# Three r buffers and two bank pairs in the first pass, a new order of its work, fewer stashes early, and a later finish in attention

## The reference

```
h = relu(layernorm(x))                       # per row
# layer 0
score = sum(h[src] * h[dst]);  a = softmax of score over the edges of one dst
agg = segment_sum((h @ W_conv + b_conv)[src] * a, dst)
out = agg + relu(h @ W_res + b_res)          # r = the second term, for all nodes
x = x + batchnorm(out)                       # mean and variance over all 100,000 rows
# layer 1
h = relu(layernorm(x))
m = gelu(gelu([h[src], h[dst], edge_attr] @ W_m1 + b_m1) @ W_m2 + b_m2)
boxes = segment_sum(m, dst)
x = x + gelu(gelu([h, boxes] @ W_c1 + b_c1) @ W_c2 + b_c2)
```

## Time and profile before

| what | value |
|---|---|
| median of 3 runs | 1633.65 us (1632.19 to 1642.5) |
| the profiled execution | 1630.99 us, of which the span of its instructions is 1629.2 us |
| first pass, until VectorE's last instruction of it | 0 to 312.2 us |
| VectorE idle until the first edge rows are there | 312.2 to 329.3 us |
| attention and the batch norm's numbers | 329.3 to 722.5 us |
| dense pass | 722.5 to about 1180 us |
| edge pass | about 1180 to 1629 us |
| VectorE busy in the first pass, in attention | 260.16 of 312.2 us, 340.65 of 393.2 us |
| TensorE's granted clock in the two | 0.83, 0.76 of full speed |

### The profile page before, as it was taken

One profiled execution on the slowest core, in us unless ns is written; L12 is line 12 of the kernel. 1 busy time (PEld: TensorE's weight loads), 2 busy tenths in 40 slices (PEclk: granted clock), 3 DMA queues, 4 the chain that ended last, 5 costly groups with the idle time before them and its releaser, 6 DMA issues.

```text
span 1629.2 us, 21884 instructions
## 1 busy us (share of the span) xinstructions
PE 1290.4 (79%) x6227; PEld 777.5 (48%) x6227; DVE 1234.1 (76%) x2432; ACT 945.8 (58%) x1647; POOL 1093.4 (67%) x989
## 2 busy tenths in 40 slices
PE   4566665558778778767999989999969999999983
PEld 2233332247666667654545444444444454554431
DVE  8898888488988988866777777777667777777661
ACT  5688786623323323326777777777646676666651
POOL 7788887777777777777776057667735555445355
PEclk8888788757877877878999999999989999999985
DMA  7666675468876543354655467666375454454410
GB/s 211 222 224 195 206 221 199 146 223 294 275 275 221 142 124 115 91 194 139 203 185 192 163 209 230 202 202 201 113 230 151 142 159 133 143 158 130 123 50 16
DMA packets 141969, 287.34 MB, mean 176 GB/s; under 512 B 33104, under 2 KB 50614, under 8 KB 141852
## 3 DMA queue, kind: packets, MB, share of 16 engines
q1 hardware_dynamic: 109532, 255.32, 46.9%
q0 software_dynamic: 32320, 30.62, 8.0%
HBM read 165.47 MB, written 121.80 MB: 176 GB/s over the span
## 4 chain that ended last, share of the span: by engine, by line
PE 47%; DVE 18%; POOL 16%; issue 10%; ACT 6%; DMA 2%; SPq 0%; DVEq 0%; POOLq 0%; ACTq 0%
POOL x_ring L607 8%; POOL gout L607 7%; PE banks L1501 6%; PE banks L1478 6%; PE banks L1525 4%; PE banks L1407 3%; PE banks L1598 3%; PE banks L1596 3%; PE banks L1424 3%; PE banks L1605 3%; PE banks L1511 3%; DVE sums L841 3%; ACT cT L1230 2%; DVE gout L1016 2%; PE banks L1491 2%
## 5 line engine op out<-in xcount | busy, mean ns | idle before, releaser
L607 POOL DMA_INDIRECT agg_ring<-agg_rows,edge_idx x196 | 213.5, 1089 | 161.4 <-DMA edge_agg<-agg_ring 97.5
L611 POOL DMA_INDIRECT out<-agg,put_last x196 | 196.5, 1002 | 184.3 <-DVE agg L1048 129.3
L607 POOL DMA_INDIRECT x_ring<-in_x,edge_idx x200 | 239.2, 1196 | 63.5 <-issue 63.5
L607 POOL DMA_INDIRECT gout<-in_x,edge_idx x192 | 226.2, 1178 | 58.5 <-issue 58.2
L611 POOL DMA_INDIRECT agg_rows<-agg,put_first x196 | 216.9, 1107 | 59.7 <-issue 55.8
L738 DVE TENSOR_REDUCE stat<-sq 128x16 f32<-128x1024 f32 (+1 forms) x98 | 118.7, 1213 | 26.3 <-ACT sq L1093 21.9
L1229 ACT ACTIVATE cT<-banks,packed 96x512 f32<-96x512 f32 (+1 forms) x98 | 66.8, 682 | 107.4 <-PE banks L1501 107.3
L963 DVE TENSOR_TENSOR xc<-banks,xc 128x512 f32<-128x512 f32 (+1 forms) x74 | 51.2, 692 | 92.2 <-PE banks L1525 90.9
L1501 PE MATMUL banks<-hT,packed 64*96 64x512 f32 (+1 forms) x392 | 112.6, 652 | 2.8 <-ACT hT L1222 2.8
L1365 PE MATMUL banks<-ident,xc 128*128 128x128 f32 (+1 forms) x296 | 54.4, 345 | 75.9 <-DVE xc L767 64.9
L1511 PE MATMUL banks<-cT,packed 96*64 96x512 f32 (+1 forms) x392 | 105.5, 616 | 0.4 <-ACT gout L1238 0.4
(11 more groups left out here) (191 smaller groups left out, 3384.8 us busy)
## 6 DMA issues: line engine op xcount, KB each, us to landing
xt<-in_x SPq DMA_DIRECT2D x48, 512.0 KB, 6.1
r_rows<-rT SPq DMA_DIRECT2D x48, 512.0 KB, 7.0
xe<-edge_x SPq DMA_DIRECT2D x96, 256.0 KB, 3.8
agg_rows<-rb SPq DMA_DIRECT2D x48, 512.0 KB
xt<-in_x_t SPq DMA_DIRECT2D x36, 512.0 KB, 5.0
out<-xc SPq DMA_DIRECT2D x36, 512.0 KB, 3.2
edge_r<-rr SPq DMA_DIRECT2D x48, 256.0 KB, 3.8
rT<-r_rows SPq DMA_DIRECT2D x24, 512.0 KB, 5.6
```

The lines of the kernel that those rows point to most:

```text
L607: A.indirect_dma_start(to, None, table[:, :], bass.IndirectOffsetOnAxis(ap=idx, axis=0), bounds_check=limit, oob_is_err=False).then_inc(si ...
L611: A.indirect_dma_start(table[:, :], bass.IndirectOffsetOnAxis(ap=idx, axis=0), rows_of, None, bounds_check=limit, oob_is_err=False).then_i ...
```

## The change

In the first pass r has three buffers instead of two (the third is rb[0]) and three store semaphores. The products of even steps go to the banks W[1], of odd steps to W[3], so `r_product(s)` waits for the relu of s - 2 instead of s - 1. The unread output of `square_r` goes to the banks W[2] instead of SBUF. ACT's work on a pair of r is put off: in pair i it copies, takes the relu of and squares the steps of pair i - 1 in a new order. DVE sums, centres, sums, centres, and polishes after both. SP stores the steps 2i - 3 and 2i - 2 in pair i, and stashes up to group 6i // 7 instead of i + 1, so 20 groups in the first pass instead of 25; in attention it goes on with 6/5 of a group a pair, still with at least 2i + 6. STASH goes from 9 to 12. In attention `edge_finish` of both groups stands behind `invert`.

```
-STASH = 9
+STASH = 12
-        r_junk, zero = rb[0], rb[1]
+        r_ring = rT + rb[0:1]
+        zero = rb[1]
+        r_banks = [W[1], W[3]]
+        r_junk = W[2]
-        A_st = slots("r_stored", 2)
+        A_st = slots("r_stored", 3)
...
# SP, first pass
-                for s in (a - 2, a - 1):
+                for s in (a - 3, a - 2):
                     if is_step(s):
                         store_r(s)
-                due = i + 1
+                due = 6 * i // 7
...
# SP, attention
-            store_r(S - 1)
+            for s in (S - 2, S - 1):
+                store_r(s)
+            before = stashed
             for i in range(PAIRS + 1):
                 a = 2 * i
-                due = min(G, max(PAIRS + 4 * (i + 1) // 3, a + 6))
+                due = min(G, max(before + 6 * (i + 1) // 5, a + 6))
...
# DVE, first pass
                     sum_squares(dstat(1, s, p), sq[s % 2][0:p, :], A_sq, s, A_ss)
-                if is_step(2 * i + 2):
-                    center(2 * i + 2)
+                    if is_step(s + 2):
+                        center(s + 2)
                 polish(i, nodes_of(pair[-1]), 0, R * len(pair))
...
-                if is_step(2 * i + 3):
-                    center(2 * i + 3)
# DVE, attention (edge_center: n == 2 waits for the transposes of S - 2, not S - 1)
-                for n in (a, b):
-                    if is_group(n - 4):
-                        edge_finish(n - 4)
-                    if is_group(n):
-                        p = edges_of(group_of(n))
-                        sum_squares(estat(1, n, p), esq[n % 2][0:p, :], E_sq, n, E_ss)
                 pair = [n for n in (a, b) if is_group(n)]
+                for n in pair:
+                    p = edges_of(group_of(n))
+                    sum_squares(estat(1, n, p), esq[n % 2][0:p, :], E_sq, n, E_ss)
                 if pair:
                     invert(i, P, 2 * R, 2 * R + ER * len(pair), E_inv, E_ss, pair[-1])
+                for n in (a - 4, b - 4):
+                    if is_group(n):
+                        edge_finish(n)
...
# ACT, first pass (relu_r and square_r use r_ring[s % 3] and r_banks[s % 2], wait for s - 3)
             square(0, A_ctr, A_ss, A_sq)
-            for i in range(PAIRS + 1):
+            square(1, A_ctr, A_ss, A_sq)
+            for i in range(PAIRS):
                 a, b = 2 * i, 2 * i + 1
-                if is_step(b):
-                    square(b, A_ctr, A_ss, A_sq)
+                if is_step(a - 2):
+                    copy_hT(a - 2)
+                if is_step(b - 4):
+                    square_r(b - 4)
+                if is_step(b - 2):
+                    copy_hT(b - 2)
                 if is_step(a - 2):
                     relu_r(a - 2)
-                if is_step(a):
-                    last = b if is_step(b) else a
-                    seed_roots(i, nodes_of(last), 0, R * (last - a + 1), last)
+                last = b if is_step(b) else a
+                seed_roots(i, nodes_of(last), 0, R * (last - a + 1), last)
+                if is_step(a + 2):
+                    square(a + 2, A_ctr, A_ss, A_sq)
+                if is_step(b - 2):
+                    relu_r(b - 2)
                 if is_step(a - 2):
                     square_r(a - 2)
-                if is_step(a + 2):
-                    square(a + 2, A_ctr, A_ss, A_sq)
-                if is_step(a - 1):
-                    relu_r(a - 1)
-                    square_r(a - 1)
-                for s in (a, b):
-                    if is_step(s):
-                        copy_hT(s)
+                if is_step(b + 2):
+                    square(b + 2, A_ctr, A_ss, A_sq)
...
# ACT, start of attention
+            copy_hT(S - 1)
+            square_r(S - 2)
             for n in range(2):
                 square_group(n)
+            relu_r(S - 1)
+            square_r(S - 1)
...
# PE (r_product: W[1] becomes r_banks[s % 2])
-                A_relu.part(pe, s - 1, b + 1)
+                A_relu.part(pe, s - 2, b + 1)
...
             pe.wait_ge(s_b, 12)
+            A_relu.done(pe, S - 2)
+            A_rsq.done(pe, S - 1)
```

More of the change, by code:

```diff
@@ L403, in store_r @@
                 p = nodes_of(s)
-                o, i = r_rows[s], rT[s % 2][:, :]
+                o, i = r_rows[s], r_ring[s % 3][:, :]
                 if p != P:
@@ L812, in edge_center @@
                 if n == 2:
-                    A_t.done(dve, S - 1)
+                    A_t.done(dve, S - 2)
                 subtract_mean(ec[n % 4][0:p, :], xe[n % 4][0:p, :], estat(0, n, p), E_ctr, n, 1)
@@ L1111, in relu_r @@
                 p = nodes_of(s)
-                A_st.done(act, s - 2)
-                A_rsq.done(act, s - 2)
+                A_st.done(act, s - 3)
+                A_rsq.done(act, s - 3)
                 for b in range(2):
@@ L1116, in relu_r @@
                     act.wait_ge(A_r.sem, A_r.after(s, b + 1))
-                    A.activation(blocks(rT[s % 2][:, c], p), blocks(W[1][:, c], p), ACT.Relu, bias=bres2[:, :],
+                    A.activation(blocks(r_ring[s % 3][:, c], p), blocks(r_banks[s % 2][:, c], p), ACT.Relu, bias=bres2[:, :],
                                  accum_out=rsum[:, 2 * s + b:2 * s + b + 1]).then_inc(A_relu.sem, 1)
@@ L1123, in square_r @@
                 A_rsq.done(act, s - 1)
[L1124 removed]
+                A.activation(blocks(r_junk[:, :], p), blocks(r_ring[s % 3][:, :], p), ACT.Square,
                              accum_out=rsq[:, s:s + 1]).then_inc(A_rsq.sem, 1)
             square(0, A_ctr, A_ss, A_sq)
[L1128 removed]
+            square(1, A_ctr, A_ss, A_sq)
+            for i in range(PAIRS):
                 a, b = 2 * i, 2 * i + 1
[L1130 to L1131 removed]
+                if is_step(a - 2):
[4 more added lines that the diff above has]
+                    copy_hT(b - 2)
                 if is_step(a - 2):
                     relu_r(a - 2)
[L1134 to L1136 removed]
+                last = b if is_step(b) else a
[4 more added lines that the diff above has]
+                    relu_r(b - 2)
                 if is_step(a - 2):
                     square_r(a - 2)
[L1139 to L1146 removed]
+                if is_step(b + 2):
+                    square(b + 2, A_ctr, A_ss, A_sq)
             def edge_square(n, p, ready, summed, st):
@@ L1372, in r_product @@
                 pe.wait_ge(A_ht.sem, A_ht.after(s, b + 1))
-                A_relu.part(pe, s - 1, b + 1)
-                T.matmul(blocks(W[1][:, c], p), wres2[:, :], blocks(hT2[s % 2][:, c], p), start=True, stop=True)\
+                A_relu.part(pe, s - 2, b + 1)
+                T.matmul(blocks(r_banks[s % 2][:, c], p), wres2[:, :], blocks(hT2[s % 2][:, c], p), start=True, stop=True)\
                  .then_inc(A_r.sem, 1)
```

1 line of the change is left out of this document (removed).

## The result

| kernel | median (lowest to highest, runs) | profiled execution's span |
|---|---|---|
| before | 1632.92 us (1629.95 to 1642.5, 4) | 1629.2 us |
| changed | 1616.36 us (1613.91 to 1619.69, 4) | 1612.1 us |

A forecast was written before the change was run, and what follows sets the result against it. POOL's unpausing gathers, 12.66 us a group with one stash a pair, were taken to bound the first pass. 1630.99 - 35 - 12.7 - 10 = 1573.3 us profiled, so a median of 1576, range 1555 to 1604.

The forecast's parts named there:

- first pass's mechanism: First pass: fewer stashes due let DVE set the pace instead of POOL's gathers; -35 us, bounds -38 and -15.
- under 30: First pass, sign in the trace: SP's waits for gathers under 30 us instead of 171.8.
- 7 us of waits for seeds: First pass: of 42.0 us, about 4.5 stay in the last pair and 2.5 over the others.
- no pair is faster than 12.66 us: First pass before the change: SP stashes one group a pair, and a group's gathers take 12.66 us.
- Handover: From first pass to attention: DVE's 17.10 us wait for the first edge rows shrinks; -12.7 us (-15 to -9).
- Now nothing on SP waits for a gather there: Handover: the first edge rows' loads no longer stand behind stash and gather of the 25th group.
- rival (1): First pass: POOL sets the pace again, a group taking 12.95 us; +12 us, 1588 in total; chance 0.13.
- the lead: First pass: POOL starts more than a group ahead, so its 10.85 us a pair doesn't hold DVE before the last pairs.
- Attention: Attention: moving edge_finish removes DVE's wait for the product; twelve slow pairs at 0.8 us, -10 us, bounds -29 and +10.
- the slack of 0.8 us a slow pair: Attention's slow pairs: PE has half the next scan's transposes at 500.2 us, the scan started at 501.04.
- Cost nothing: Later passes: first stash of sums due at 936 us, when POOL has had its four groups since 906; no cost.
- Dense pass: Dense pass: as long as before, a forecast difference of 0.

The follow-up runs named there:

- g4: Changed kernel with the old pace of gathered groups (one a pair in the first pass, 4/3 in attention): 2044.3 us, 1.014 of the kernel before.
- i3: Changed kernel with a shorter pause after each indirect DMA, STASH 10, and first-pass row sums and roots in PSUM: 1688.1 us, 1.035 of the kernel before.
- g1: The changed kernel itself, nothing altered, on a slower chip: 2047.6 us, 1.022 of the kernel before.
- g2: Changed kernel with STASH 10 in place of 12, on a slower chip: 2021.5 us, 1.012 of the kernel before.
- f2: Changed kernel with first-pass row sums and polished roots in PSUM, so one SBUF input: 2111.9 us, 1.039 of the kernel before.
- f3: Changed kernel with one SBUF input in the first pass and STASH 10: 2096.1 us, 1.031 of the kernel before.
- e3: Changed kernel with edge_finish back in its old place between the square sums: 2063.9 us, 1.024 of the kernel before.
- e2: Changed kernel with STASH 9 as before: 2029.1 us, 1.009 of the kernel before.
- f4: Changed kernel with edge_finish back in its old place, repeated on the second chip: 2082.8 us, 1.025 of the kernel before.
- f1: Changed kernel with STASH 10, on the second chip: 2065.3 us, 1.014 of the kernel before.
- i1: Changed kernel with a shorter pause (memset of 128 x 320) after each indirect DMA, on a chip like the first: 1693.7 us, 1.040 of the kernel before.
- i2: Changed kernel with the shorter pause after each indirect DMA and STASH 10: 1709.2 us, 1.050 of the kernel before.
- e4: The kernel before with STASH 12 alone: 2037.5 us, 1.013 of the kernel before.

## Why the prediction was wrong

- **The first pass's mechanism was right, and its size within the bounds.** 10.36 us a pair against 10.53 worked out, SP's waits for gathers 26.3 against "under 30", none of ACT on r's store in the steady pairs. The 4.3 us that lack are the start and the end: the forecast left 7 us of waits for seeds, and 14.1 are there. From 36.6 to 56 us SP waited 19.6 us for rows that VectorE builds (17.4 before), with r's stores behind it, and VectorE then stood 5.8 us for seeds at 71.4 us (a reach that the forecast didn't follow); the last three pairs' seeds come 1.5, 2.8 and 3.5 us late. g4 shows that none of this gain is there without the pace. One reading of the working is wrong without harm: "no pair is faster than 12.66 us". From 83.3 to 162.8 us the pairs of the kernel before took 11.4 us each; 12.66 is a mean, and the sum used it as one.
- **Handover, -7.9 for -12.7.** "Now nothing on SP waits for a gather there" fell. Gathers were priced at 12.66 us a group as before, but denser two-input instructions hold them longer: 1.41 + 0.30 us, 13.6 us a group. This is rival (1)'s mechanism, at 0.95 us a group and not the 0.29 it was given, and it did not set the steady pace, as the lead covered it until the last pairs. i3 measured what it costs there on the paced kernel: 9.9 us with the end of the first pass.
- **Attention, -3.2 for -10.** That the wait moves to the scan was foreseen; the slack of 0.8 us a slow pair was not there: 22.9 us in 12 waits stand where 24.5 stood. The two-pair period fell from 30.91 to 30.72 us, and a slow pair from 16.64 to 16.47 where 15.8 was forecast. The step priced the slack with TensorE's 14.64 us of the old slow pair, as if the clock there stayed at 0.59. It is 0.53 now, and 14.47 us are busy with fewer products; the clock is lower in the fast pair too (0.94 for 1.00). Why was not tested. The finish in its old place gave 2063.9 and 2082.8 us, ratios of 1.024 and 1.025 where the changed kernel on another chip has 1.022 +-0.012: nothing that these runs can tell, so that no experiment shows what the move is worth.
- **"Cost nothing" for the stashes of sums: the step that failed, and the largest part of the miss.** It asked whether the first stash, at 936 us by its count (956.27 measured), finds its four groups, and stopped there. It had to ask as well whether the last ones are in HBM when the edge pass reads them, a pass that was to begin 58 us earlier: with three groups a pair from 12 instead of 9 the sums came 4.6 us earlier, the pass 35.4. Measured cost +18.3 us, beside 21.9 us more of VectorE's waits for sums. On the slower chips STASH 12 against 9 or 10 costs 27 to 34 us of edge pass: g1/g2 and f2/f3, where nothing else differs and the pass starts within 3 us, and e3/e2, f4/f1, where the finish differs too (and f1's pass starts 27 us later, which takes from the last figure). The pair i1/i2 says nothing of it.
- **Dense pass, +6.4 us**: TensorE's clock there is 0.96 for 0.97, with 8 falls of the clock instead of 4, about 1.6 us each (an estimate from 18 us stretches at a clock of 0.91); TensorE is busy 424.0 us there for 417.5. Why there are more was not tested.

The errors add up: 4.3 + 4.8 + 6.8 + 6.4 + 18.3 = 40.6 us, which is the forecast's distance. Without the edge pass's 18.3 us the forecast would have been 22.3 us off. The changed kernel with STASH at 10 and no pause was never run on a chip like the first; that it would give the 18 us back is argued (GpSimd's ring is full some 18 us after its first gather at 890.5 us, and a first stash two pairs ahead of 956.3 us, at 18.3 us a pair, goes out near 920), not shown. No version beat both kernels on both sorts of chip: the pause wins 0.876 on one and loses 1.040 on the other.

## What to carry to other kernels

When a queue's duty is put off, follow it to both ends: to the first item (is it there when it is due?) and to the last (is it there when it is read?), and find who stands with a full buffer in between. A duty with a fixed place in a pass has to move by as much as the passes around it do. Where VectorE's denser work held the gathers, a group went from 12.66 to 13.6 us; price such work at the density after the change. And a wait that ends an instruction group moves to the next dependency on the same engine unless that one has slack of its own: measure the slack at the new place, not the wait at the old.

## What the runs showed of the hardware

- An indirect gather takes 1.00 us beside VectorE's reductions and 1.74 to 1.91 us beside its 1.22 us instructions with two SBUF inputs; with one of the inputs in PSUM it takes 1.00 us throughout (996 and 1003 ns of mean). The Trainium skill, SBUF — State Buffer, "Who interferes with whom", says that a VectorE instruction with two SBUF inputs contends with a GpSimd instruction that reads SBUF; the runs agree. The held gather ends 0.86 to 0.88 us after that instruction, also where a second such instruction follows at once (the gather at 208.39 us).
- Chips differ: of the five numbered ones, one takes 1631 us for the kernel before, as the first comparison's did, and four take 1990 to 2060. On the slower sort, indirect DMAs 1.28 to 1.30 us apart bring the other engines nearly to a stand (TensorE busy 7.8 of 43 us, where it was 33.5 on the first chip), and a pause of 0.49 us after each takes 208 us off the kernel before; on the faster sort the same DMAs cost the others nothing that shows.
- So a change can lose on one chip what it wins on another: 0.988 and 1.022 here. STASH 12 alone costs the kernel before 1.013 on a chip of the slower sort (e4); what makes up the rest was not taken apart.
- TensorE's clock did not stay where it was when VectorE's order changed: in attention the slow pair went from 0.59 to 0.53 and the fast one from 1.00 to 0.94, and the two together took 30.7 us for 30.9. Why was not tested.
